# Gathers of two edge attentions released chunk by chunk, norm stages ordered by tile, a placing step with two digits

## The chip, the cores and the metric

The kernel runs on one core of one Trainium2 chip. The metric is the device time of one execution in microseconds (us); less is better. The engines are named as in the profile: PE (TensorE, with PEld for its weight loads), DVE (VectorE), ACT (ScalarE), POOL (GpSimd) and SP (the queue that issues most DMAs). A suffix q (SPq, POOLq) means an instruction of the engine's queue that occupies no data path.

## The reference

A graph of 3125 nodes with 256 features each; the edges are 25000 random pairs in both directions and one loop per node, 53125 in all, sorted by target. Four layers, each as `x = layernorm(x + f(x))`:

```python
# layer 0: attention, 8 heads; scores from text embeddings, values from x
scores = sum(Q[col] * (K[row] + rel)) / sqrt(32);  attn = softmax over the edges of each target
out = segment_sum(attn * V[row]) @ Wo.T + bo
# layer 1: attention, 4 heads; score = leaky(alpha_src[src] + alpha_dst[dst])
h = segment_sum(softmax(score) * val[src])
# layer 2: 5 GIN layers  (segment_sum(relu(h[src])), two products, two batch norms each)
# layer 3: 3 SAGE layers (mean over neighbours, two products)
```

All inputs and the output are float32.

## The kernel before

The program is a row of phases. Each is closed by a barrier of all engines (class Phase), and within one each engine runs its own list of instructions in order, with waits on semaphores written by hand. The order is: prepare, find_windows, attend_edges and merge_parts for layer 0, residual_norm (norm 0), tables_layer1, attend_edges for layer 1, merge_parts, residual_norm (norm 1), GIN, norm 2, SAGE, norm 3.

**attend_edges** (from L554; once per attention). The edges are cut into 416 chunks of 128, and 8 chunks make one of 52 groups. A buffer `from_src` holds the gathered rows of RING = 4 groups. For each chunk POOL issues one indirect DMA (L682) that brings the 128 source rows from HBM: 2 KB a row in layer 0 (values and keys), 1056 B in layer 1 (values and alphas). SP loads a window of 128 target rows for each chunk (L663). A function `tick` on each engine handles one group g, and the steps of neighbouring groups are interleaved:

- PE sums the eight chunks of group g - 1 (`sum_parts`, L854 and L856: values and weights times a one-hot matrix) into two PSUM buffers that alternate by chunk. ACT copies each sum out (L945, L947), and PE may start chunk j only when ACT has copied chunk j - 2. The last matmul of a chunk increments `chunk_summed[b]`, b being the buffer of the group.
- PE turns the scores of group g (L835), DVE runs two scans for the largest score of each target (L734, L737), PE turns the result back (L841), DVE subtracts (L746, L749), ACT takes the exponent (L929, L930), and DVE weights the gathered values (L753).
- DVE makes the one-hot matrices of group g + 2 (L695, L696), PE turns them (L805), ACT copies them (L922).
- PE spreads the target rows of group g + 1 to its edges (L827). In layer 0 DVE multiplies them by the gathered keys (`match`, L707) and reduces to scores (L719); in layer 1 it adds the alphas (L725, L728).
- In layer 1 DVE, PE and ACT count the edges into an adjacency matrix beside it (L769, L771, L869, L960).

POOL has only the gathers there. For group g it waits once, for the eighth chunk of group g - 4, whose buffer it reuses, and then issues eight gathers in one block:

```python
for g in range(NG):
    b = g % RING
    pool.wait_ge(chunk_summed[b], G * (g // RING) + 1)
    for j in range(G):
        nc.gpsimd.indirect_dma_start(...).then_inc(src_in[b], 16)
```

The waits for the first four groups are met at the start. A gathered group is first read two ticks after the tick in which its gathers are released.

**prepare** (from L84). A loop over 25 node tiles makes the tables of layer 0 on PE (L369). In the same loop each edge chunk's target number is placed into a table of parts: DVE makes one-hots of the tile (`is_tile`, L297) and of the row (`is_row`, L301) for 16 chunks, POOL multiplies the first by the digits of the target number (`tile_digits`, L211), and PE multiplies the two (L358). The number is carried as three float16 digits: number / 64, number mod 64, and a flag for a part that spans chunks.

**residual_norm** (from L1310; four times). 25 tiles of 128 nodes in five slabs of five tiles. For a slab, x is summed with what is added (norm 0: the attention's result turned and multiplied by Wo, L1527, L1468, L1535; norms 2 and 3: the turned h_t, turned back by PE, L1497), DVE takes the statistics (L1418, L1421, L1423), ACT the square root (L1449), DVE the shift (L1429, L1431), ACT normalises (L1454), and PE and ACT turn the result (L1506, L1460). In norm 0 PE also makes the alphas (L1513). Each engine handles one step for a whole slab before the next step: PE, for example, projects the tiles of slab s + 2, then turns out slab s, then makes the alphas of slab s - 1. The order on ACT is root(s + 1), copy_more(s + 2), normalise(s), copy_turned(s).

## Time and profile before

| | |
|---|---|
| time, median of 3 runs (lowest to highest) | 4185.14 us (4184.43 to 4191.37) |
| the profiled execution's own time | 4209.37 us |
| its span, first to last instruction | 4207.7 us, 54657 instructions |
| PE busy | 3086.4 us (73%) |
| DVE, ACT, POOL busy | 1658.5, 1079.9, 1138.7 us |
| phases: prepare, find_windows | 0 to 188, to 272 |
| attention 0, merge, norm 0, tables of layer 1 | to 1270, 1326, 1431, 1490 |
| attention 1, merge, norm 1 | to 2482, 2553, 2593 |
| GIN, norm 2, degrees, SAGE, norm 3 | to 3548, 3596, 3603, 4172, 4207 |

Times in the profile are us from the first instruction unless marked ns. A row in order of time has the start, the duration, the engine, the line, the operation, output <- inputs and how many were merged (xN), and in brackets the idle time of the engine before it and what ended it. What ended a wait is inferred from the semaphores, and where a number of a semaphore is used again in another phase the name can be that of an old transfer. A row of busy time has the stretch and its length, then the busy us (and instructions) of PE, PEld, DVE, ACT and POOL, then the clock that PE was granted as a share of 2.4 GHz, the mean busy share of the core's 16 DMA engines, and GB/s moved. The end of a matmul in the profile is modelled from its size; it is not the time at which other engines see its result. The page also lists, by line, the time spent busy, the mean of one instruction, and the idle time before it.

### The profile page before, as it was taken

Reading aid. Unit: us, or ns where it says so; the run is one execution under the profiler, and the core shown is the slowest. Engines: PE = TensorE matmul, PEld = TensorE weight load, DVE = VectorE, ACT = ScalarE, POOL = GpSimd, SP = SyncE. Lnnn points to the kernel's source line nnn. Section 1 sums busy time; section 2 is a strip of 40 time slices with the busy share of each in tenths; the row PEclk is TensorE's granted clock in tenths of the full one; section 3 lists DMA queues with packets and bytes.
Section 4 is the critical chain, followed back from the end, with each engine's and each line's share of the span. In section 5 each row is a group of like instructions: output and inputs, shape, how many; then the busy total and the mean of one; then the engine's idle time right before and its main releaser. Section 6 shows DMA issues by size and latency. Waiting matters only on the chain. (4 is left out here: it accounts for less than half of the span.)

```text
span 4207.7 us, 54657 instructions
## 1 busy us (share of the span) xinstructions
PE 3086.4 (73%) x17789; PEld 2267.0 (54%) x17789; DVE 1658.5 (39%) x2726; ACT 1079.9 (26%) x2952; POOL 1138.7 (27%) x1072
## 2 busy tenths in 40 slices
PE   5306666666675646666666675999999997799997
PEld 4305565565563536655565663555555564455554
DVE  8725455455554134444444444141323324302112
ACT  0002233233331224443443433030322313201001
POOL 6563443434433243434434321000000000101010
PEclk8758888888886667777877776999999998899998
DMA  5255555555543134444544334424233240433331
GB/s 205 63 168 155 175 172 160 176 160 175 173 128 101 47 77 83 77 78 88 84 83 79 78 56 143 153 91 134 92 105 113 89 144 0 146 114 101 102 131 42
DMA packets 330861, 477.67 MB, mean 114 GB/s; under 512 B 148534, under 2 KB 241414, under 8 KB 329940
## 3 DMA queue, kind: packets, MB, share of 16 engines
q1 hardware_dynamic: 271492, 297.49, 25.4%
q0 software_dynamic: 59088, 176.67, 14.7%
q8 instruction: 148, 2.42, 0.2%
q14 instruction: 133, 1.09, 0.1%
HBM read 417.29 MB, written 58.52 MB: 113 GB/s over the span
## 5 line engine op out<-in xcount | busy, mean ns | idle before, releaser
L854 PE MATMUL e_part_ps<-e_onehot,e_from_src 128*128 128x129 f32 x3328 | 674.5, 335 | 601.3 <-ACT ends L947 349.0
L854 PEld LDWEIGHTS e_part_ps<-e_onehot,e_from_src 128*128 128x128 f32 x3328 | 560.5, 235 | 678.3 <-ACT ends L947 391.6
L945 ACT ACTIVATE sums<-e_part_ps 128x384 f32 x832 | 410.3, 493 | 1115.9 <-PE e_part_ps L856 356.8
L682 POOL DMA_INDIRECT e_from_src<-vk,src x416 | 394.3, 948 | 583.4 <-PE e_part_ps L856 454.1
L682 POOL DMA_INDIRECT e_from_src<-val,src x416 | 394.4, 948 | 578.9 <-PE e_part_ps L856 444.5
L2060 PE MATMUL gin_sum_ps<-slab,high 128*128 128x391 f16 x2000 | 497.7, 330 | 2.5 <-DMA slab<-adj 1.8
L2060 PE MATMUL gin_sum_ps<-slab,low 128*128 128x391 f16 x2000 | 497.4, 330 | 0.0
L827 PE MATMUL e_spread_ps<-e_window,e_onehot_t 128*128 128x256 f32 (+1 forms) x1664 | 346.8, 346 | 63.8 <-DMA e_window<-q_part 28.7
L856 PE MATMUL e_part_ps<-e_onehot,e_small 128*65 128x129 f32 x1664 | 382.3, 318 | 0.0
L827 PEld LDWEIGHTS e_spread_ps<-e_window,e_onehot_t 128*128 128x128 f32 x1664 | 269.2, 208 | 85.2 <-issue 41.6
L1754 PE MATMUL sage_sum_ps<-slab,high 128*128 128x391 f16 x1200 | 301.1, 333 | 11.7 <-DVE z_t L1877 6.4
L1754 PE MATMUL sage_sum_ps<-slab,low 128*128 128x391 f16 x1200 | 301.3, 333 | 0.0
L2060 PEld LDWEIGHTS gin_sum_ps<-slab,low 128*128 128x128 f16 x2000 | 195.0, 97 | 139.4 <-issue 1.8
L734 DVE TENSOR_TENSOR_SCAN e_fixed<-link,e_turn_ps 64x128 f32<-64x128 bf16 x104 | 43.8, 421 | 568.2 <-DMA out<-pr_zero 492.5
L2060 PEld LDWEIGHTS gin_sum_ps<-slab,high 128*128 128x128 f16 x2000 | 194.9, 98 | 131.2 <-DVE low L2229 4.6
L856 PEld LDWEIGHTS e_part_ps<-e_onehot,e_small 128*65 128x65 f32 x1664 | 257.3, 167 | 0.0
L753 DVE TENSOR_TENSOR e_from_src<-e_from_src,e_fixed 128x2048 f32<-128x2048 f32 x104 | 237.9, 2288 | 43.2 <-ACT e_fixed L929 41.6
L2122 POOL TENSOR_SCALAR h_t<-h_t 128x391 f32<-128x391 f32 x32 | 39.7, 1251 | 780.3 <-DVE h_t L2267 780.3
L2237 DVE SCALAR_TENSOR_TENSOR z_t<-h_t,gin_own,gin_sum_ps 128x391 f32<-128x391 f32 x80 | 44.8, 617 | 490.1 <-PE gin_sum_ps L2060 490.1
L2131 ACT ACTIVATE gin_y_t<-gin_proj_ps,gin_columns 128x391 f32<-128x391 f32 x80 | 46.8, 585 | 572.6 <-PE gin_proj_ps L2073 572.6
L707 DVE TENSOR_TENSOR e_from_src<-e_from_src,e_spread_ps 128x512 f32<-128x512 f32 x208 | 140.5, 675 | 121.4 <-PE e_spread_ps L827 105.0
L1877 DVE TENSOR_TENSOR z_t<-sage_sum_ps,inv_degree_all 128x391 f32<-128x391 f32 x48 | 23.8, 558 | 364.3 <-PE sage_sum_ps L1754 364.3
(282 smaller groups left out, 4255.4 us busy)
## 6 DMA issues: line engine op xcount, KB each, us to landing
slab<-adj SPq DMA_DIRECT2D x160, 977.5 KB, 4.8
e_window<-q_part SPq DMA_DIRECT2D x416, 128.0 KB
adj<-e_counts SPq DMA_DIRECT2D x8, 1250.0 KB
adj<-e_counts SPq DMA_DIRECT2D x8, 1193.8 KB
e_from_src<-vk,src POOLq DMA_INDIRECT x416
e_from_src<-val,src POOLq DMA_INDIRECT x416
e_window<-alpha_part SPq DMA_DIRECT2D x416, 4.0 KB
vk<-pr_out SPq DMA_DIRECT2D x25, 256.0 KB, 2.0
```

What stands on the lines that cost most here:

```text
L682: nc.gpsimd.indirect_dma_start(from_src[:, b, j, :], None, by_src, bass.IndirectOffsetOnAxis(ap=keep["src"][:, g * G + j:g * G + j + 1], a ...
L707: nc.vector.tensor_tensor(k_rows, k_rows, spread_ps[pair % 2][:, :].rearrange("p (j d) -> p j d", j=2), ALU.mult).then_inc(used[pair % 2], 1)
L734: nc.vector.tensor_tensor_scan(running, keep["link"][:, g, 0:P], turned, -FAR, ALU.add, ALU.max).then_inc(fwd, 1)
L753: nc.vector.tensor_tensor(from_src[:, b, :, 0:D].rearrange("p j (h d) -> p j h d", h=H), from_src[:, b, :, 0:D].rearrange("p j (h d) -> p ...
L827: mm = nc.tensor.matmul(to, onehot_t[:, r, j, :], window[:, r, j, :], start=True, stop=True)
L854: nc.tensor.matmul(part_ps[s][:, k * ENDS:(k + 1) * ENDS], from_src[:, b, j, k * P:(k + 1) * P], onehot[:, b, j, :], start=True, stop=True)
L856: nc.tensor.matmul(part_ps[s][0:SMALL, KH * ENDS:(KH + 1) * ENDS], small[:, r, j, :], onehot[:, b, j, :], start=True, stop=True).then_inc( ...
L945: nc.scalar.activation(keep["sums"][:, :, bass.ds(starts[j], P)], of[:, :, 0:P], ACT.Copy).then_inc(whole_copied, 1)
L1754: mm = nc.tensor.matmul(sum_ps[KH * n + m][:, 0:AN], part[:, t, m * P:(m + 1) * P], slab[:, s, n, k * AN:(k + 1) * AN], start=(t == 0 and ...
L2060: mm = nc.tensor.matmul(sum_ps[KH * n + m][:, 0:AN], part[:, t, m * P:(m + 1) * P], slab[:, s, n, k * AN:(k + 1) * AN], start=(t == 0 and ...
L2131: nc.scalar.activation((z_t if p else y_t)[:, m, cols(b)], proj_ps[v % (2 * KH)][:, 0:AN], ACT.Identity, bias=columns[:, 3 * p, m:m + 1], ...
L2237: nc.vector.scalar_tensor_tensor(out=z_t[:, m, cols(b)], in0=h_t[:, m, cols(b)], scalar=own[:, l:l + 1], in1=sum_ps[KH * n + m][:, 0:AN], ...
```

## The change

In `attend_edges`, each gather waits for the sum of its own chunk in the group four back, not once for the last of the eight. In `prepare`, the flag is added to the second digit as 64, two digits are multiplied and placed, and the flag is taken out again afterwards by one comparison and one subtraction. In `residual_norm`, PE, ACT and DVE go tile by tile: PE and ACT bring in tile t + 7 (SLAB + AHEAD) between the steps of tile t, the copy of a turned tile follows the normalising of the next, the alphas follow by tile, and DVE takes the statistics of a tile right after its sum, the bias being added to the slab ahead of it; the shift of slab s - 1 is made after the second tile of slab s. In norm 1, where nothing is turned in, the sum stays by slab and the shift of slab s - 1 comes before it.

```diff
-            pool.wait_ge(half_sem, 5)
+            pool.wait_ge(half_sem, 4)
             for u in range(STEPS):
                 cols = slice(u * STEP, (u + 1) * STEP)
                 if u >= 2:
                     pool.wait_ge(placed, u - 1)
                 pool.wait_ge(tiles_spotted, u + 1)
                 nc.gpsimd.tensor_tensor(tile_digits[:, u % 2, :, :, :],
-                                        is_tile[:, u % 2, :, :].unsqueeze(2).to_broadcast([P, STEP, 3, TW]),
-                                        digits[:, cols, :].unsqueeze(3).to_broadcast([P, STEP, 3, TW]), ALU.mult).then_inc(digits_spotted, 1)
+                                        is_tile[:, u % 2, :, :].unsqueeze(2).to_broadcast([P, STEP, 2, TW]),
+                                        digits[:, cols, :].unsqueeze(3).to_broadcast([P, STEP, 2, TW]), ALU.mult).then_inc(digits_spotted, 1)
...
-            nc.vector.tensor_copy(digits[:, :, 1], ints[:, 5, :]).then_inc(half_sem, 1)
...
-            nc.vector.tensor_tensor(spans[:, 0, :], spans[:, 0, :], spans[:, 1, :], ALU.add).then_inc(spanned, 1)
+            nc.vector.tensor_tensor(spans[:, 0, :], spans[:, 0, :], spans[:, 1, :], ALU.max).then_inc(spanned, 1)
             v.wait_ge(spanned, 5)
-            nc.vector.tensor_tensor(digits[:, :, 2], spans[:, 0, :], keep["first"][:, :], ALU.mult).then_inc(half_sem, 1)
+            nc.vector.scalar_tensor_tensor(out=spans[:, 0, :], in0=spans[:, 0, :], scalar=64.0, in1=keep["first"][:, :],
+                                           op0=ALU.mult, op1=ALU.mult).then_inc(spanned, 1)
+            v.wait_ge(spanned, 6)
+            nc.vector.tensor_tensor(digits[:, :, 1], spans[:, 0, :], ints[:, 5, :], ALU.add).then_inc(half_sem, 1)
...
+            nc.vector.tensor_scalar(part_number[:, 2, :], part_number[:, 1, :], 63.5, None, ALU.is_gt).then_inc(node_sem, 1)
+            v.wait_ge(node_sem, 3)
+
+            nc.vector.scalar_tensor_tensor(out=part_number[:, 0, :], in0=part_number[:, 2, :], scalar=-64.0,
+                                           in1=part_number[:, 0, :], op0=ALU.mult, op1=ALU.add).then_inc(node_sem, 1)
+            v.wait_ge(node_sem, 4)
...
-                    mm = nc.tensor.matmul(node_ps[:, 0:3 * TW], is_row[:, u % 2, j, :],
+                    mm = nc.tensor.matmul(node_ps[:, 0:2 * TW], is_row[:, u % 2, j, :],
...
             for g in range(NG):
-                b = g % RING
-
-                pool.wait_ge(chunk_summed[b], G * (g // RING) + 1)
+                b, it = g % RING, g // RING
                 for j in range(G):
+
+                    if it:
+                        pool.wait_ge(chunk_summed[b], G * (it - 1) + j + 2)
                     nc.gpsimd.indirect_dma_start(
                         from_src[:, b, j, :], None, by_src,
                         bass.IndirectOffsetOnAxis(ap=keep["src"][:, g * G + j:g * G + j + 1], axis=0)).then_inc(src_in[b], 16)
...
+            def add_tile(t):
+
+                if by_tile:
+                    v.wait_ge(in_turned, t + 1)
+                    nc.vector.tensor_tensor(x[:, t, :], x[:, t, :], in_ps[t % IN][:, 0:D], ALU.add).then_inc(summed, 1)
+                v.wait_ge(summed, t + 1 if by_tile else t // SLAB + 1)
+                nc.vector.bn_stats(stats[:, t, :], x[:, t, :]).then_inc(stat, 1)
...
-            take_stats(0)
-            for s in range(1, NSLAB):
-                take_stats(s)
-                make_shift(s - 1)
+            for s in range(NSLAB):
+                if s and not by_tile:
+                    make_shift(s - 1)
+                add_slab(s)
+                for t in tiles(s):
+                    add_tile(t)
+                    if s and by_tile and t % SLAB == AHEAD - 1:
+                        make_shift(s - 1)
+                close_slab(s)
...
+            if weight is not None:
+                for t in range(SLAB + AHEAD):
+                    copy_more(t)
+            for s in range(NSLAB):
+                root(s)
                 for t in tiles(s):
-                    nc.scalar.activation(x[:, t, :], x[:, t, :], ACT.Identity, bias=shift[:, t:t + 1],
-                                         scale=std[:, t:t + 1]).then_inc(normed, 1)
-
-            def copy_turned(s):
-                for t in tiles(s):
-                    act.wait_ge(out_turned, t + 1)
-                    nc.scalar.activation(turned_to[:, :, t * P:(t + 1) * P], out_ps[t % OUT][:, 0:D].rearrange("p (k n) -> p k n", k=KH),
-                                         ACT.Copy).then_inc(out_copied, 1)
-
-            def copy_more(s):
-                for t in tiles(s):
-                    act.wait_ge(more_turned, t + 1)
-                    if t >= 2:
-                        act.wait_ge(in_turned, t - 1)
-                    nc.scalar.activation(more_t[:, t % 2, :, :], turn_ps[t % 2][:, 0:D].rearrange("p (k n) -> p k n", k=KH),
-                                         ACT.Copy).then_inc(more_copied, 1)
-
-            if weight is not None:
-                copy_more(0)
-                copy_more(1)
-            root(0)
-            for s in range(NSLAB):
-                if s + 1 < NSLAB:
-                    root(s + 1)
+                    normalise(t)
+                    if turned_to is not None and t % SLAB:
+                        copy_turned(t - 1)
+                    if weight is not None and t + SLAB + AHEAD < NT and t % SLAB < SLAB - AHEAD:
+                        copy_more(t + SLAB + AHEAD)
+                if turned_to is not None:
+                    copy_turned(t)
                 if weight is not None and s + 2 < NSLAB:
-                    copy_more(s + 2)
-                normalise(s)
-                if turned_to is not None:
-                    copy_turned(s)
+                    for u in range(AHEAD):
+                        copy_more((s + 2) * SLAB + u)
...
+            def bring_in(t):
+
+                if t >= NT:
+                    return
+                if added_t is not None:
+                    turn_in(t)
+                elif weight is not None:
+                    if t + 1 < NT:
+                        turn_more(t + 1)
+                    project_in(t)
...
-            if added_t is not None:
-                turn_in(0)
             if weight is not None:
                 pe.wait_ge(w_in, 16)
-                project_in(0)
-                project_in(1)
+                turn_more(0)
+            for t in range(SLAB + AHEAD):
+                bring_in(t)
             for s in range(NSLAB):
-                if added_t is not None and s + 1 < NSLAB:
-                    turn_in(s + 1)
-                if weight is not None and s + 2 < NSLAB:
-                    project_in(s + 2)
-                if turned_to is not None:
-                    turn_out(s)
-                if alpha_to is not None and s > 0:
-                    make_alpha(s - 1)
+                for t in tiles(s):
+                    if turned_to is not None:
+                        turn_out(t)
+                    if t % SLAB < SLAB - AHEAD:
+                        bring_in(t + SLAB + AHEAD)
+                    if alpha_to is not None and t:
+                        make_alpha(t - 1)
+                for u in range(AHEAD):
+                    bring_in((s + 2) * SLAB + u)
             if alpha_to is not None:
-                make_alpha(NSLAB - 1)
+                make_alpha(NT - 1)
```

## Rows read from the trace of the kernel before

**Rows 1.** Busy time by stage (us; instructions in brackets), TensorE's clock, DMA share, GB/s:

```profile
0.00:188.00 188.00, 97.57 (x728) 78.15 (x728) 159.41 (x153) 0.00 (x0) 118.91 (x40) 0.86 0.42 144
...
1326.00:1431.00 105.00, 69.58 (x300) 56.86 (x300) 30.91 (x95) 32.30 (x82) 0.00 (x0) 0.68 0.31 99
...
3548.00:3596.00 48.00, 24.62 (x100) 17.34 (x100) 23.18 (x90) 21.62 (x55) 0.00 (x0) 0.57 0.00 0
...
4172.00:4207.00 35.00, 11.35 (x50) 8.30 (x50) 22.18 (x90) 13.76 (x30) 0.00 (x0) 0.53 0.27 92
...
400.00:1230.00 830.00, 563.70 (x3287) 490.22 (x3284) 417.33 (x530) 254.30 (x842) 338.06 (x357) 0.84 0.55 170
...
1600.00:2430.00 830.00, 543.65 (x3851) 499.04 (x3852) 381.79 (x492) 341.33 (x989) 335.19 (x354) 0.76 0.48 83
```

**Rows 2.** Costliest groups: busy, mean ns | idle before them, and its releasers:

```profile
L682 POOL DMA_INDIRECT e_from_src<-vk,src x416 | 394.3, 948 | 583.4 <-PE e_part_ps L856 454.1
...
L734 DVE TENSOR_TENSOR_SCAN e_fixed<-link,e_turn_ps 64x128 f32<-64x128 bf16 x104 | 43.8, 421 | 568.2 <-DMA out<-pr_zero 492.5
```

**Rows 3.** Order of time, one group of the second attention (start, us, engine, line):

```profile
1912.63 0.94 POOL L682 DMA_INDIRECT e_from_src<-val,src  x1 [8.39 <-PE e_part_ps L856]
...
1914.35 0.66 PE L854 MATMUL e_part_ps<-e_onehot,e_from_src 128*128 128x129 f32 x4
...
1914.79 0.22 DVE L725 TENSOR_TENSOR e_raw_score<-e_from_src,e_spread_ps 128x64 f32<-128x64 f32 x1 [1.66 <-PE e_spread_ps L827]
...
1915.07 0.61 PE L854 MATMUL e_part_ps<-e_onehot,e_from_src 128*128 128x129 f32 x4
...
1915.74 0.27 PE L835 MATMUL e_turn_ps<-ident,e_score 128*64 128x128 f32 x1
...
1921.41 0.95 POOL L682 DMA_INDIRECT e_from_src<-val,src  x1 [0.30 <-issue]
...
1924.22 0.49 ACT L945 ACTIVATE sums<-e_part_ps 128x384 f32 x1 [3.75 <-remote]
...
1924.25 0.42 DVE L734 TENSOR_TENSOR_SCAN e_fixed<-link,e_turn_ps 64x128 f32<-64x128 bf16 x1 [8.98 <-DMA out<-pr_zero]
```

**Rows 4.** Busy time around those gathers, and in a group without gathers:

```profile
1912.60:1913.90 1.30, 1.30 (x14) 1.30 (x15) 0.53 (x1) 0.72 (x4) 0.97 (x2) 1.00 0.03 1
...
1913.90:1924.00 10.10, 2.11 (x23) 1.84 (x22) 0.45 (x2) 1.35 (x2) 6.62 (x7) 0.86 0.43 109
...
1924.00:1932.60 8.60, 7.62 (x58) 7.13 (x58) 5.88 (x8) 5.54 (x17) 0.00 (x0) 0.77 0.03 2
...
334.00:343.40 9.40, 9.40 (x72) 8.43 (x71) 9.15 (x13) 4.67 (x15) 0.00 (x0) 1.00 0.37 114
```

**Rows 5.** Order of time, the next group's first two sums copied by ACT:

```profile
1936.96 0.49 ACT L945 ACTIVATE sums<-e_part_ps 128x384 f32 x1 [1.96 <-PE e_part_ps L856]
...
1941.27 0.49 ACT L945 ACTIVATE sums<-e_part_ps 128x384 f32 x1 [3.75 <-DMA x<-x]
```

**Rows 6.** Order of time, DVE and POOL in the first stage's loop:

```profile
30.71 0.64 DVE L297 TENSOR_TENSOR pr_is_tile<-pr_iota,pr_tile_of 128x464 f16<-128x464 f16 x1
...
46.76 4.45 POOL L211 TENSOR_TENSOR pr_tile_digits<-pr_is_tile,pr_digits 128x1392 f16<-128x1392 f16 x1 [0.64 <-DVE pr_is_tile L297]
...
49.67 2.03 DVE L297 TENSOR_TENSOR pr_is_tile<-pr_iota,pr_tile_of 128x464 f16<-128x464 f16 x1
...
51.85 4.45 POOL L211 TENSOR_TENSOR pr_tile_digits<-pr_is_tile,pr_digits 128x1392 f16<-128x1392 f16 x1 [0.64 <-DVE pr_is_tile L297]
```

**Rows 7.** Order of time, norm 0, the first projection of two slabs:

```profile
1356.44 2.07 PE L1535 MATMUL n_in_ps<-n_w_out,n_more_t 128*128 128x256 f32 x4 [4.78 <-ACT n_more_t L1468]
...
1373.09 2.08 PE L1535 MATMUL n_in_ps<-n_w_out,n_more_t 128*128 128x256 f32 x4 [4.78 <-ACT n_more_t L1468]
```

**Rows 8.** Order of time, norm 2, DVE's first sums of two slabs:

```profile
3562.72 2.13 DVE L1409 TENSOR_TENSOR x<-x,n_in_ps 128x256 f32<-128x256 f32 x5 [4.57 <-PE n_in_ps L1497]
...
3572.15 2.13 DVE L1409 TENSOR_TENSOR x<-x,n_in_ps 128x256 f32<-128x256 f32 x5 [4.57 <-PE n_in_ps L1497]
```

More of the change, by code:

```diff
@@ L1352, in residual_norm @@
         loads = (add is not None) + (x_from is not None)
+        by_tile = added_t is not None or weight is not None
+        AHEAD = 2
         block = ctx.enter_context(nc.Block(f"norm{layer}"))
@@ L1416, in take_stats, with close_slab @@
                     v.wait_ge(biased, s + 1)
-                for t in tiles(s):
-                    nc.vector.bn_stats(stats[:, t, :], x[:, t, :]).then_inc(stat, 1)
+                if not by_tile:
+                    nc.vector.tensor_tensor(x[:, slab, :], x[:, slab, :], more[:, slab, 0:D], ALU.add).then_inc(summed, 1)
+            def close_slab(s):
+                slab = slice(s * SLAB, (s + 1) * SLAB)
                 v.wait_ge(stat, SLAB * (s + 1))
@@ L1539, in _, with turn_in, turn_more @@
-            if added_t is not None:
-                turn_in(0)
+            def turn_in(t):
+                if t >= IN:
+                    pe.wait_ge(summed, t - IN + 1)
+                for k in range(KH):
+                    mm = nc.tensor.transpose(in_ps[t % IN][:, k * P:(k + 1) * P], added_t[:, k, t * P:(t + 1) * P], keep["ident"][:, :])
+                mm.then_inc(in_turned, 1)
+            def turn_more(t):
+                if t % SLAB == 0:
+                    pe.wait_ge(loaded[t // SLAB], 16 * loads)
+                if t >= 2:
+                    pe.wait_ge(more_copied, t - 1)
+                for k in range(KH):
+                    mm = nc.tensor.transpose(turn_ps[t % 2][:, k * P:(k + 1) * P], more[:, t, k * P:(k + 1) * P], keep["ident"][:, :])
+                mm.then_inc(more_turned, 1)
```

103 lines of the change are left out of this document (43 added, 60 removed).

## The prediction, made before the result was known

> **What bounds the kernel now.** First the busy time by stage [rows 1]. The two attentions take 998 and 992 us of the 4207.7 us span, and in them no engine is near full: in 830 us of the first PE is busy 563.7, DVE 417.3, ACT 254.3, POOL 338.1. In that window POOL issues 357 gathers, 44.6 groups of eight: one group per 18.6 us; in 830 us of the second, 354 gathers: one per 18.8 us. Next the costliest groups of instructions [rows 2]: in the first attention alone POOL waits 454.1 us for PE's chunk sums, so PE holds the gathers back, and DVE is idle 568.2 us before its first scan, 492.5 of it put down to a releaser that cannot be the right one (a store of zeros done long before). So I went to the order of time in one group [rows 3]. The gathers start at 1912.63. PE sums a chunk from 1914.35 and the next from 1915.07, 0.7 us a chunk, and turns the scores at 1915.74 for 0.27 us. DVE needs only that, but its scan starts at 1924.25, 8.2 us later; ACT, which should copy the first sum out at about 1915.3, starts at 1924.22. Both start 1.9 us after the last gather instruction has ended (1921.41 + 0.95). The busy times of the same stretches [rows 4] say what lasts until then: for 1.3 us after the first gather's start the DMA share is 0.03, then for 10.1 us it is 0.43 and PE is busy 2.1 us, DVE 0.45, ACT 1.35; then the share is 0.03 again and in 8.6 us PE does 7.6. So while the data of gathers arrives, PE's finished results are hardly seen by DVE, ACT and POOL. A few slip through: in the next group ACT copies the first sum at 1936.96, in the midst of the gathers, and the second only at 1941.27 [rows 5]. A group without gathers takes 9.4 us, and PE is busy in all of it at the full clock of 2.4 GHz [rows 4]. So a group of today is 9.4 us of work and then about 10 us of gathers, nearly one after the other: 9.4 + 10.1 = 19.5 against 18.7 measured.
>
> The Trainium skill, page "SBUF — State Buffer", section "Who interferes with whom", says that DMA never contends with a compute engine. By that rule the wait has another cause and it does not matter when a gather is in flight. The rows disagree in time at least: PE's results come out when the traffic ends. I weigh the rule as the first rival below.
>
> **The change, part by part.**
>
> *Gathers one chunk at a time (both attentions).* The same 416 gathers each, none added; a gather now waits for the sum of its own chunk four groups back, not for the eighth. The first four groups need no wait, as before, and the last three have no gathers behind them, so 48 periods per attention change, 96 in all. POOL gains seven waits a group; it queues nothing else there, and no consumer is near: the gathered group is used two groups later. So an earlier gather is worth nothing by itself. What changes is that eight gathers in one block become several short ones between the sums. Take each block with its sums as a round. PE's results are seen up to about 2 us after a gather's start (1.3 us until traffic, and DVE's L725 started 2.2 us after it [rows 3]); after the last gather of the block they are all seen. One gather's data takes (1924.0 - 1913.9) / 8 = 1.26 us, and its tail ends 2.8 us after its start (1.9 + 0.95). Let two sums be seen at time 0. Gathers start at 0 and 1.25. ACT copies the first sum out (0.49 + 0.17), PE needs 0.7 for the next, so a third sum is done at about 1.4: seen, and a third gather joins. The fourth, after ACT's second copy, is done at about 2.0 to 2.2: even chance. The fifth is not seen before the block ends at 2.5 + 2.8 = 5.3 (with the fourth inside: 6.6). A round of three sums in 5.3 us is 14.1 us for eight, of two in 4.05 us (third missed) 16.2, of four in 6.6 us 13.2. To that come the results that are not sums: turned scores, turned peaks, spread windows, turned one-hots; each that falls into a block is late by what is left of it, at most about 3 us now instead of 8.2, but DVE's 9.4 us of work in a group (417.3 / 44.6 [rows 1]) must fit around them. Also PE falls to 1.2 GHz now and then (clock 0.84 and 0.76 of full [rows 1]), which stretches 9.4 us of work. I add 1 to 2 us to the 14.1 and take 15.7 us. Gain: 18.7 - 15.7 = 3.0 us x 96 = 288 us. The ends: PE's own work, 9.4 us a group, would give 9.3 x 96 = 893 us; eight blocks of one, none beside any work, would cost 9.4 + 8 x 1.5 = 21.4 us (a single gather's stall taken as its tail less the free head, 2.8 - 1.3), 2.7 x 96 = 259 us more than now. I stay near the middle, since the row of the first 2 us and the rows of the rest of the block are from the same kernel and only their order is new.
>
> *Two digits in place of three (prepare).* The loop turns once in 5.09 us (POOL L211 at 46.76 and 51.85 [rows 6]), 25 times. DVE's is_tile takes 0.64 us before POOL runs at all and 2.03 beside it, ending at 51.70, 0.5 us after POOL's 46.76 + 4.45 = 51.21: it waits for POOL's multiply, and POOL's next waits for it: 4.45 + 0.64 = 5.09. With 928 in place of 1392 elements I take POOL at two thirds, 2.97 us, so 3.61 us a turn; DVE's own work is 5.09 - 2.03 + 0.64 = 3.70, and that binds next. PE has 97.6 us in the whole stage [rows 1], 3.9 a turn at most. I take 3.85: gain 1.24 x 25 = 31 us. Ends: 36 (3.64), and 15 if POOL has a fixed part. The two added small DVE operations ahead of the loop lie beside DVE's wait for inputs; the two behind it cost 0.4 us.
>
> The Trainium skill, same page, section "SBUF: two separate sides", calls the port pair that DVE and GpSimd share an exclusive lock held for the whole instruction. The 0.5 us between POOL's end and is_tile's end agree with it; by a split of bandwidth instead, the loop would still be bound by POOL and the sum the same.
>
> *Norm 0 by tile.* A slab of five tiles takes 16.65 us (PE L1535 at 1356.44 and 1373.09 [rows 7]), and in each PE waits 4.78 us for ACT, which stands in its queue at the square root that DVE makes ready; DVE then waits for PE's last tile behind five turns. The same instructions are now interleaved by tile, seven tiles ahead. PE has 69.6 us in the 105, at a clock of 0.68. I take PE's wait away in four slabs (19 us) and at the end, where turns and alphas follow the last five tiles, two tiles of PE's work (69.6 / 25 = 2.8 us each): 25 us. Ends: 36 (PE never idle) and 5.
>
> *Norm 2* takes 9.43 us a slab [rows 8], with DVE idle 4.57 of it behind normalise, turn, copy, turn in. DVE's own 4.9 us and about 1 us for the waits on its own results by tile give 6.7: gain 2.7 x 4 = 11 us (3 to 16). *Norm 3* has no turning back; DVE has 22.2 of 35 us; 3 us (0 to 6). *Norm 1* moves only the order of ACT and PE, and what it waits for is its loads: nothing, 3 us either way.
>
> **Sum.** 288 + 31 + 25 + 11 + 3 = 358 us off the profiled execution's 4209.4 us, 3851 us. That execution is 24.2 us (0.58%) above the median 4185.1, so by the same factor: 3830 us.
>
> **Rivals.**
> *A: order does nothing in the attentions.* What is late is late because eight gathers have to pass in a period, whenever they do; the period stays 18.7. For it: the work and the traffic add up today to nearly the period, and the page's rule above. Against it: idle engines beside short blocks have what to do, and today's block is idle because it is long. Time: (4209.4 - 70) x 0.994 = 4115 us.
> *B: the overlap is nearly full.* Results come through between short blocks, as one did at 1936.96; the period goes to 11 to 14 us, where DVE's 9.4 and PE's 9.4 us bind. At 12.8: 5.9 x 96 = 566, time 3550 us.
> *C: slower.* Each gather, released by its own sum, makes its own stall, just as the results that the next sum needs are due: the place is ACT's copy between a sum and the sum two further on. Eight stalls with nothing beside them give 21.4 us: 4209 - 70 + 259 = 4398, by the same factor 4373 us. It decides from a period of 18.7 + 70 / 96 = 19.4 us on. For it: traffic would then cover nearly all of the period, where today 8.6 us are quiet, and PE may lose its clock in many short idle times (at 1.2 GHz its 9.4 us are 18.8). Against it: PE and ACT can always go one pair of sums further while one gather lands, and the other stages give 70 us in any case.
>
> **How the numbers follow.** Forecast (period 14.2 to 17.3, 3690 to 3985 us) 0.50; A and between (17.3 to 19.4) 0.21; B 0.18; C 0.09; within 0.2% of before 0.02. A measurement of this kernel tells about 0.2% from no change. The range 3610 to 4130 us takes in all of A and the upper part of B (a period from 13.4 us on), and leaves out C. Faster 0.89, same 0.02, slower 0.09.
>
> **What would show it.** Right: gathers start at uneven distances, two to four together; the scan L734's idle time falls from 5.5 us each (568.2 us over 104 [rows 2]) to under 3; the period of L682 by eights is near 15.7; DMA share in the attentions rises by a fifth with the same bytes; L211 near 3 us and its distance 3.85; norm 0 near 80 us. Wrong: if the stalls are not tied to traffic, ACT and DVE would again start together once a group; and if PE's clock in the attentions falls below 0.7, C is the case.

## The result: 3600 us, a gain 1.6 times the forecast, the excess all in the attentions

The changed kernel takes 3600.32 us (median of 4 runs, 3586.49 to 3608.12) against 4185.03 us: a ratio of 0.8596, interval 0.8568 to 0.8624. The forecast was 3830 us, the range 3610 to 4130. Its profiled execution took 3598.55 us, with a span of 3596.8 us. From barrier to barrier in the two profiles:

| stage | before, us | after, us | gain | forecast |
|---|---|---|---|---|
| prepare | 187.9 | 171.8 | 16.1 | 31 |
| attention 0 | 997.4 | 703.6 | 293.8 | 144 |
| attention 1 | 992.3 | 731.8 | 260.5 | 144 |
| norm 0 | 105.4 | 76.0 | 29.4 | 25 |
| norm 1 | 39.2 | 40.8 | -1.6 | 0 |
| norm 2 | 47.8 | 39.7 | 8.1 | 11 |
| norm 3 | 35.4 | 34.9 | 0.5 | 3 |
| the rest | 1801.8 | 1797.8 | 4.0 | 0 |

Busy time by stage in the profile after (stretch, its length, busy us of PE, PEld, DVE, ACT, POOL, TensorE's clock, DMA share, GB/s); it answers [rows 1]:

```profile
0.00:172.00 172.00, 90.69 (x728) 71.84 (x728) 138.64 (x155) 0.00 (x0) 98.40 (x40) 0.86 0.47 158
1016.00:1092.00 76.00, 52.75 (x300) 45.58 (x300) 32.63 (x95) 32.23 (x82) 0.00 (x0) 0.81 0.44 137
400.00:900.00 500.00, 422.56 (x2923) 359.44 (x2922) 367.04 (x471) 228.80 (x750) 298.55 (x316) 1.00 0.81 250
1200.00:1800.00 600.00, 488.06 (x3901) 446.83 (x3901) 384.58 (x495) 340.92 (x994) 338.22 (x359) 0.89 0.66 112
```

In the first attention 316 gathers fall into 500 us: 12.66 us for eight, where it was 18.6. PE is busy 0.85 of the time instead of 0.68, and its granted clock went from 0.84 to 1.00; in the second attention from 0.76 to 0.89. The DMA share of the first attention went from 0.55 to 0.81, a rise by a half with the same bytes where a fifth was forecast, as the period fell by more than was forecast. The costliest groups after; they answer [rows 2]:

```profile
L690 POOL DMA_INDIRECT e_from_src<-vk,src x416 | 393.1, 945 | 290.7 <-PE e_part_ps L864 184.3 <-issue 86.1 <-POOLq L74 16.9
...
L690 POOL DMA_INDIRECT e_from_src<-val,src x416 | 393.0, 945 | 318.5 <-PE e_part_ps L864 219.6 <-issue 75.7 <-POOLq L74 20.5
...
L742 DVE TENSOR_TENSOR_SCAN e_fixed<-link,e_turn_ps 64x128 f32<-64x128 bf16 x104 | 43.8, 421 | 131.0 <-PE e_turn_ps L843 76.7 <-issue 37.7 <-DMA out<-pr_zero 16.6
```

The scan's idle time is 1.3 us each instead of 5.5. The order of time in one group of the first attention after (start, us, engine, line) shows how; it answers [rows 3, 5]:

```profile
685.86 0.95 POOL L690 DMA_INDIRECT e_from_src<-vk,src  x1 [1.47 <-PE e_part_ps L864]
...
686.09 0.27 PE L843 MATMUL e_turn_ps<-ident,e_score 128*64 128x128 f32 x1
...
686.40 0.42 DVE L742 TENSOR_TENSOR_SCAN e_fixed<-link,e_turn_ps 64x128 f32<-64x128 bf16 x1 [0.83 <-issue]
...
687.11 0.95 POOL L690 DMA_INDIRECT e_from_src<-vk,src  x1 [0.30 <-issue]
...
687.60 0.38 PE L864 MATMUL e_part_ps<-e_onehot,e_small 128*65 128x129 f32 x2
...
688.36 0.95 POOL L690 DMA_INDIRECT e_from_src<-vk,src  x1 [0.30 <-issue]
...
690.18 0.49 ACT L953 ACTIVATE sums<-e_part_ps 128x384 f32 x1 [2.25 <-PE e_part_ps L864]
...
690.33 0.95 POOL L690 DMA_INDIRECT e_from_src<-vk,src  x1 [1.02 <-PE e_part_ps L864]
...
691.58 0.95 POOL L690 DMA_INDIRECT e_from_src<-vk,src  x1 [0.30 <-issue]
...
692.84 0.95 POOL L690 DMA_INDIRECT e_from_src<-vk,src  x1 [0.30 <-issue]
...
695.01 0.94 POOL L690 DMA_INDIRECT e_from_src<-vk,src  x1 [1.23 <-PE e_part_ps L864]
```

The scores turned at 686.09 are scanned at 686.40: at once. The sum that PE ended at 687.98 (687.60 + 0.38) is copied at 690.18, 2.2 us late. So the hold (PE has finished a result, and the other engines see it late) is still there, but a block has two or three gathers (685.86, 687.11, 688.36; then 690.33, 691.58, 692.84). POOL goes on 1.97 and 2.17 us after the last start of a block, 0.7 and 0.9 us more than the 1.25 us inside a block.

In prepare, norm 0 and norm 2 the periods are read in the same way; they answer [rows 6, 7, 8]:

```profile
40.95 3.65 POOL L211 TENSOR_TENSOR pr_tile_digits<-pr_is_tile,pr_digits 128x928 f16<-128x928 f16 x1 [0.64 <-DVE pr_is_tile L299]
...
45.25 3.66 POOL L211 TENSOR_TENSOR pr_tile_digits<-pr_is_tile,pr_digits 128x928 f16<-128x928 f16 x1 [0.65 <-DVE pr_is_tile L299]
...
1036.97 0.60 ACT L1473 ACTIVATE x<-x,n_shift,n_std 128x256 f32<-128x256 f32 x1 [2.87 <-DVE n_shift L1445]
...
1049.26 0.60 ACT L1473 ACTIVATE x<-x,n_shift,n_std 128x256 f32<-128x256 f32 x1 [2.95 <-DVE n_shift L1445]
...
2957.36 0.42 DVE L1412 TENSOR_TENSOR x<-x,n_in_ps 128x256 f32<-128x256 f32 x1 [1.84 <-PE n_in_ps L1518]
...
2964.33 0.42 DVE L1412 TENSOR_TENSOR x<-x,n_in_ps 128x256 f32<-128x256 f32 x1 [1.84 <-PE n_in_ps L1518]
```

### The profile page after: what moved, and what is told of

It is laid out like the page before. It is cut to its first block and busy times, and to the rows that moved or that the text cites. A ratio compares the mean times of both kernels' runs of the same rounds, so it can differ in the third digit from the quotient of the medians.

```text
span 3596.8 us, 54659 instructions
## 1 busy us (share of the span) xinstructions
PE 2896.4 (81%) x17789; PEld 2083.4 (58%) x17789; DVE 1637.8 (46%) x2728; ACT 1081.6 (30%) x2952; POOL 1115.2 (31%) x1072
## 5 line engine op out<-in xcount | busy, mean ns | idle before, releaser
L862 PE MATMUL e_part_ps<-e_onehot,e_from_src 128*128 128x129 f32 x3328 | 588.4, 302 | 177.0 <-issue 95.4
L862 PEld LDWEIGHTS e_part_ps<-e_onehot,e_from_src 128*128 128x128 f32 x3328 | 473.4, 202 | 252.3 <-issue 136.8
L835 PE MATMUL e_spread_ps<-e_window,e_onehot_t 128*128 128x256 f32 (+1 forms) x1664 | 325.9, 330 | 101.8 <-DMA e_window<-q_part 39.0
L864 PE MATMUL e_part_ps<-e_onehot,e_small 128*65 128x129 f32 x1664 | 337.3, 286 | 0.0
L835 PEld LDWEIGHTS e_spread_ps<-e_window,e_onehot_t 128*128 128x128 f32 x1664 | 258.2, 203 | 129.7 <-issue 76.3
L761 DVE TENSOR_TENSOR e_from_src<-e_from_src,e_fixed 128x2048 f32<-128x2048 f32 x104 | 237.6, 2284 | 18.5 <-issue 12.4
L864 PEld LDWEIGHTS e_part_ps<-e_onehot,e_small 128*65 128x65 f32 x1664 | 222.2, 147 | 0.0
L1783 PEld LDWEIGHTS sage_sum_ps<-slab,high 128*128 128x128 f16 x1200 | 117.1, 98 | 89.8 <-issue 13.8
```

Of the source, the lines that this page charges most:

```text
L761: nc.vector.tensor_tensor(from_src[:, b, :, 0:D].rearrange("p j (h d) -> p j h d", h=H), from_src[:, b, :, 0:D].rearrange("p j (h d) -> p ...
L835: mm = nc.tensor.matmul(to, onehot_t[:, r, j, :], window[:, r, j, :], start=True, stop=True)
L862: nc.tensor.matmul(part_ps[s][:, k * ENDS:(k + 1) * ENDS], from_src[:, b, j, k * P:(k + 1) * P], onehot[:, b, j, :], start=True, stop=True)
L864: nc.tensor.matmul(part_ps[s][0:SMALL, KH * ENDS:(KH + 1) * ENDS], small[:, r, j, :], onehot[:, b, j, :], start=True, stop=True).then_inc( ...
L1783: mm = nc.tensor.matmul(sum_ps[KH * n + m][:, 0:AN], part[:, t, m * P:(m + 1) * P], slab[:, s, n, k * AN:(k + 1) * AN], start=(t == 0 and ...
```

## The experiments

The runs fell on four chips, and that matters: on chips 7, 8 and 4 the kernel before takes 4183 to 4216 us, as on the chip of the first profiles, and on chip 11 3382 us. One number is used throughout, the lateness: how long after the modelled end of the last matmul of a chunk's sum its semaphore is incremented, in the first attention (third quartile over the 416 sums; where records of increments are missing, the next one is taken). In the kernel before it is 2.9 us, after the change 1.4 us. The median in the kernel before is 0.01 us, since more than half of the sums are seen at once. The number shows that there is a hold; it is not a price, since a sum made earlier also waits longer. "Period" is the distance of gathers by eights.

| run | chip | us | kernel before there | ratio, interval | period 0, 1 | lateness, us |
|---|---|---|---|---|---|---|
| e1_release_only | 11 | 3360.1 | 3381.7 | 0.9943, 0.9926 to 0.9961 | 10.1, 10.7 | 0.01 |
| e2_rest_only | 11 | 3326.6 | 3381.7 | 0.9844, 0.9828 to 0.9861 | 10.6, 10.8 | 0.01 |
| e3_pairs | 11 | 3317.0 | 3381.7 | 0.9807, 0.9785 to 0.983 | 10.1, 10.7 | 0.01 |
| e4_fours | 11 | 3319.1 | 3381.7 | 0.9813, 0.979 to 0.9836 | 10.2, 10.9 | 0.01 |
| e8_changed_again | 7 | 3605.5 | 4182.7 | 0.8618, 0.8601 to 0.8635 | 12.7, 13.4 | 1.4 |
| e9_release_only | 7 | 3650.7 | 4187.6 | 0.8723, 0.8681 to 0.8766 | 12.6, 13.2 | 1.6 |
| e18_rest_only | 4 | 4166.7 | 4215.9 | 0.9881, 0.9859 to 0.9902 | 18.6, 18.6 | 2.9 |
| e5_pauses | 7 | 3609.9 | 4182.7 | 0.863, 0.8607 to 0.8654 | 13.2, 13.5 | 1.3 |
| e10_pairs | 7 | 3628.3 | 4187.6 | 0.8662, 0.864 to 0.8685 | 12.7, 13.8 | 1.7 |
| e11_fours | 7 | 3714.6 | 4187.6 | 0.887, 0.8831 to 0.8908 | 13.8, 14.4 | 0.9 |
| e12_short_pauses | 7 | 3631.7 | 4187.6 | 0.8657, 0.8624 to 0.8689 | 13.3, 13.8 | 1.6 |
| e6_thin | 7 | 4127.7 | 4182.7 | 0.9868, 0.9841 to 0.9895 | 18.5, 18.3 | 2.1 |
| e14_half_rows | 8 | 4165.4 | 4189.7 | 0.994, 0.9921 to 0.996 | 18.6, 18.6 | 2.8 |
| e15_direct | 8 | 3701.8 | 4189.7 | 0.8834, 0.8816 to 0.8852 | none | 0.01 |
| e7_none | 7 | 3356.3 | 4182.7 | 0.8024, 0.8002 to 0.8046 | none | 0.01 |
| e13_third_buffer | 8 | 3604.3 | 4189.7 | 0.8604, 0.8578 to 0.8629 | 12.5, 13.5 | 2.4 |
| e16_two_pauses | 4 | 3719.7 | 4215.9 | 0.8829, 0.881 to 0.8847 | 15.0, 13.9 | 2.2 |
| e17_two_pauses_third | 4 | 3653.0 | 4215.9 | 0.8653, 0.8625 to 0.8682 | 13.5, 14.1 | 1.5 |

**The parts alone, and other block sizes.** In the kernel before, the wait of each gather alone (e1, e9); in the changed kernel, the wait of the block alone (e2, e18), or a wait for each two or four chunks (e3, e10 and e4, e11). The edit of the pairs:

```diff
+                    if it and j % 2 == 0:
+                        pool.wait_ge(chunk_summed[b], G * (it - 1) + j + 3)
```

> The kernel before with the chunk-by-chunk release alone. In the profiles the two attentions went from 997 and 992 us to 704 and 732 us, 554 us together, while the stages around them gave 57 us. Theory P (pauses): PE's results reach the other engines in the pauses between short blocks of gathers, and the release alone makes these; so the attentions are as in the changed kernel, within 10 us each, and the time is 4185 - 554 = 3631 us, 3610 to 3650. Rival Q: a part of the 554 us comes from what the other parts of the change leave behind (PE's clock, granted 0.82 and 0.76 before and 0.96 and 0.87 after); then the time is over 3700 us.

> The changed kernel with the gathers released in blocks of eight again: prepare and the norms are as changed. Theory P: the attentions are as in the kernel before, 990 to 1000 us each, and the 57 us of the other stages remain: 4185 - 57 = 4128 us, 4118 to 4138. Rival Q: the attentions too are shorter than before, by 50 us or more together, and the time is under 4080 us.

> The changed kernel with a release for each two chunks (after the sum of the second). Theory P: the blocks hold two or four gathers; a block of two makes a round of 1.25 + 2.2 = 3.5 us (14.0 us for eight), a block of four one of 3.75 + 2.2 = 6.0 us (12.0 us); a period of 12.5 to 14.0 us against 12.6 and 13.3 in the changed kernel, a time of 3600 to 3700 us. Rival R (what pays is that a gather follows its own sum at once): each doubling of the block costs about a third of the way back to 18.6 us, so 14.6 us and 3790 us or more.

> The changed kernel with a release for each four chunks. Theory P: two blocks of four in a group; what PE may sum ahead of ACT's copies is two chunks, so after each block about two more sums must be made before the next one: 3.75 + 2.2 + 1.4 = 7.3 us, 14.7 us a period (14 to 16), attentions of about 800 us, a time of 3750 us (3690 to 3870). Rival S (what is held back is in proportion to the gathers in flight, however they are cut): what separates the changed kernel from the one before is not the number of pauses, and fours stay close to eights: over 17 us, over 3980 us.

All four missed, since chip 11 has no hold. Busy time and order of time of e2_rest_only there, blocks of eight:

```profile
300.00:800.00 500.00, 493.70 (x3496) 426.78 (x3495) 432.92 (x565) 268.17 (x898) 358.37 (x379) 1.00 0.92 298
```

```profile
703.51 0.95 POOL L689 DMA_INDIRECT e_from_src<-vk,src  x1 [0.30 <-issue]
...
704.04 0.38 PE L863 MATMUL e_part_ps<-e_onehot,e_small 128*65 128x129 f32 x2
...
704.54 0.49 ACT L952 ACTIVATE sums<-e_part_ps 128x384 f32 x1 [1.67 <-PE e_part_ps L863]
...
704.76 0.94 POOL L689 DMA_INDIRECT e_from_src<-vk,src  x1 [0.30 <-issue]
```

The sum that ended at 704.42 is copied at 704.54, in the midst of eight gathers; 379 gathers take 500 us, 10.6 us for eight, and PE is busy 0.99 of it. There the release moves the kernel by 0.6% (e1), the other parts by 1.6% (e2). The changed kernel was then run again, unedited:

> The changed kernel once more. The four runs so far ran on another chip than the two profiles: there the kernel before takes 3382 us, its attentions 561 and 592 us, and no result of PE is held back. Theory H (the hold belongs to the chip, and the change's gain in the attentions exists only where the hold does): where the kernel before takes about 3382 us, the changed one takes 3310 to 3330 us, a ratio of 0.980 to 0.985; where it takes about 4185 us, 3590 to 3610, 0.860. Rival T (the first profiles were of some passing condition, not of a chip): a ratio between these, or 4185 us on the chip of the first four runs.

(The 561 us there is the first attention of e1; with blocks of eight it is 578.) On chip 7 the ratio is 0.862, as at first. Theory H stands as far as it was tried; the changed kernel itself was not run on chip 11. The same edits on chips with the hold:

> The kernel before with the chunk-by-chunk release alone, wanted on a chip with the hold (kernel before near 4185 us). Theory P: the attentions take 704 and 736 us as in the changed kernel, so 4185 - 550 = 3635 us (3620 to 3660). Rival Q (the other parts help the attentions): over 3700 us. On a chip without the hold: 3360 us, as measured there.

> The changed kernel with the gathers released in blocks of eight, wanted on a chip with the hold (kernel before near 4185 us), where only variants of it have run so far. Prepare and the norms alone: attentions 990 to 1000 us each, 4185 - 57 = 4128 us, 4118 to 4138. Rival Q (these parts change the attentions too): under 4080 us.

Attentions of 702 and 729 us with the release alone (3650.7 us, as P said), 997 and 995 us without it (e18). So the whole gain of the attentions is the release's: 4187.6 - 3650.7 = 537 us; the other parts gave 49 us on chip 4. The time of e18, 4166.7, lies above the 4138 of the expectation, because the kernel before took 4215.9 us on that chip, 31 us more than on the first; the attentions are as expected.

> The changed kernel with a release for each two chunks, wanted on a chip with the hold. There, blocks of eight with three pauses of 1.0 us had a period of 13.2 us in which POOL never waited. Theory P: blocks of two and four, 12.3 to 13.5 us a group, 3590 to 3680 us. Rival R (the own sum): 14.6 us and 3790 us or more. On a chip without the hold: 3317 us, as measured there.

> The changed kernel with a release for each four chunks, wanted on a chip with the hold. Theory P: two blocks of four; after each, two more sums have to be made before the next one: 3.75 + 2.2 + 1.4 = 7.3 us, 14.7 us a group (14 to 16), 3800 us (3730 to 3930). Rival S (held time in proportion to the gathers, however they are cut): over 17 us, over 4000 us. On a chip without the hold: 3319 us, as measured there.

Pairs came as P said in time (3628) and in the first attention; the second has 13.8 us, 0.3 above P's range. Fours were better than P (3715 against 3730 to 3930): all 96 blocks of each attention are of four, but in the first attention only one of the two pauses of a group is long, 3.9 us from start to start in the median, and the other 2.4 us. S is out.

**Pauses without the release.** The edit is that of e5. Groups of eight, released at the eighth sum as before, but POOL fills a small buffer of its own three times (e5) or twice (e12) after the second, fourth and sixth gather, or three times after the third and sixth (e16), the last also with a third PSUM buffer for the sums of layer 0 (e17):

```diff
+                    if j % 2 == 1 and j < G - 1:
+                        for _ in range(3):
+                            nc.gpsimd.memset(idle[:, 0:256], 0.0).then_inc(idled, 1)
+                            n_idle += 1
+                            pool.wait_ge(idled, n_idle)
```

> The changed kernel with blocks of eight, and POOL idling about 1.1 us (three small fills of a buffer of its own) after the second, fourth and sixth gather. Theory P: on a chip with the hold PE's results come through in these pauses, so that the period falls from 18.6 to 15 to 17 us although POOL does 3.3 us more in each group: 3780 to 3980 us against 4128 for blocks of eight. Rival R (it is the release after the own sum that pays): the period grows to 21.9 us, 4440 us. On a chip without the hold both say POOL's 10.0 us and 3.3 us more, 13.3 us a group: 3326 + 96 x 3.0 = 3610 us.

> The changed kernel with blocks of eight and POOL idling 0.7 us (two small fills) after the second, fourth and sixth gather, where three fills gave a pause of 1.03 us, a period of 13.2 us and 3610 us. Theory P1 (POOL's own time binds, a pause of 0.7 us lets enough through): 10.0 + 3 x 0.7 = 12.1 us, 3610 - 96 x 1.0 = 3515 us. Theory P2 (results get through only behind a gap of about 1 us): the short pauses are lost, 19 to 21 us a group, over 4100 us. Between them (some pauses fail): 13 to 16 us. On a chip without the hold 12.1 us and 3520 us by all.

POOL in e5, first attention:

```profile
503.17 0.95 POOL L692 DMA_INDIRECT e_from_src<-vk,src  x1 [0.27 <-POOL e_idle L697]
504.43 0.95 POOL L692 DMA_INDIRECT e_from_src<-vk,src  x1 [0.30 <-issue]
505.37 1.06 POOL L697 MEMSET e_idle<- 128x256 f32 x3
506.70 0.95 POOL L692 DMA_INDIRECT e_from_src<-vk,src  x1 [0.27 <-POOL e_idle L697]
507.96 0.95 POOL L692 DMA_INDIRECT e_from_src<-vk,src  x1 [0.30 <-issue]
509.21 0.95 POOL L692 DMA_INDIRECT e_from_src<-vk,src  x1 [0.30 <-issue]
```

This is the run that decides. POOL does 3.1 us more in each group, and the kernel is 573 us faster than the one before, as fast as the changed one; between two groups (507.96 to 509.21) POOL does not wait, as at 45 of the 48 group ends of the first attention and 36 of the second, so the eighth sum is done in time although no gather was released early. R is out. P predicted 3780 to 3980 and forecast too little, like the prediction itself. Pauses of 0.66 us more than the 1.26 us (e12) lose a part: in the first attention POOL waits again before half of the groups (24 of 48), 3.9 us from start to start on the mean, and the period is 13.3, not 12.1 (P1) and not 19 (P2).

> The changed kernel with blocks of eight and POOL idling 1.03 us (three fills) after the third and the sixth gather: two pauses in place of three. Wanted on a chip with the hold. With three pauses POOL never waited in the first attention (13.2 us = 8 x 1.25 + 3 x 1.03 + 0.1) and the time was 3610 us. Theory P1 (two pauses are still enough to get all results out): 12.1 us a group, 3610 - 80 = 3530 us, a version better than the changed kernel. Rival F (each pause lets about two sums through, so two pauses and the end are too few): POOL waits before each group again, 13.5 to 16 us, 3640 to 3880 us. On a chip without the hold 12.1 us, 3520 us.

> The same with three PSUM buffers for the chunk sums of layer 0. Theory P1: POOL is the bound in both, so within 10 us of the run with two pauses. Rival F: with blocks of three and three buffers three sums go through each pause in layer 0, its attention falls to 12.1 us a group (about 670 us) while layer 1 stays: 40 to 90 us under the run with two pauses.

> The changed kernel with three PSUM buffers in place of two for the chunk sums of layer 0 (layer 1 has no room), so that PE may sum three chunks ahead of ACT's copies. Wanted on a chip with the hold. Theory P (a pause ends when the sum that POOL waits for has been made and seen, and PE is stopped in a block by its two buffers): PE has three sums ready at a pause, blocks of three to four, the first attention's period falls from 12.66 to 11.5 to 12.2 us, 25 to 55 us in all, so 3550 to 3580 us. Rival B (the blocks are ended by other waits, and two buffers were not what stopped PE): within 8 us of 3603 us. On a chip without the hold POOL's 10.0 us bind: 3310 to 3330 us by both.

Two pauses are too few (F): in layer 0 POOL waits before half of the groups (24 of 48), 7.1 us from start to start on the mean, and the period is 15.0 us. With the third buffer it falls to 13.5 us, the attention from 800 to 728 us and the time by 67 us, as F said (40 to 90); F's 12.1 us and 670 us were not reached, and layer 1, where nothing was changed, went from 13.9 to 14.1 us. So in layer 0 what one pause lets through is limited in part by the two sums that PE may have ready. Where the release times the pauses itself (e13) a third buffer gave 10 us in that attention and nothing in the time: there three pauses come of themselves, and B holds. None of these beat the changed kernel.

**What in a gather holds PE's results.** Edits of the kernel with blocks of eight, from the fifth group on: rows cut to an eighth (e6), half the rows (e14), direct loads by SP of as many rows of the same length, but adjacent ones (e15), nothing (e7). All four leave the values of real sources out.

```diff
-                        from_src[:, b, j, :], None, by_src,
+                        from_src[:, b, j, 0:wide], None, table,        # e6: wide = ws // 8
...
+                    sp.dma_start(from_src[:, b, j, :], by_src[at:at + P, :]).then_inc(direct_in[b], 16)   # e15
```

> The changed kernel with blocks of eight, where from the fifth group on a gather brings only the first eighth of each row (256 and 132 bytes in place of 2048 and 1056), as many rows as before; the values used are old ones. Theory N (what holds PE's results back goes with the number of rows or with POOL's issuing, not with bytes; the two layers have the same period, 18.6 us, with rows of 2048 and 1056 bytes): on a chip with the hold the period stays 18 to 19 us, 4100 to 4150 us. Rival D (it is the data's own traffic): the period falls to 10.6 to 13 us, 3350 to 3600 us. On a chip without the hold POOL's 10.0 us bind: 3300 to 3330 us by both.

> The changed kernel with blocks of eight, where from the fifth group on each gather brings 64 rows in place of 128, of full length; the values used for the rest are old ones. Wanted on a chip with the hold (an eighth of the bytes at 128 rows changed nothing there: 4128 us). Theory N1 (the hold goes with the number of rows in flight): half the rows leave the queue idle for half of each gather's 1.25 us, results get through, a period of 10.6 to 14 us, 3370 to 3700 us. Rival N2 (it goes with POOL's issuing, whatever it issues): 18 to 19 us, 4100 to 4150 us. On a chip without the hold 3300 to 3330 us by both.

Busy time of e6, e14 and e18 in the first attention, in this order:

```profile
400.00:1200.00 800.00, 542.75 (x3176) 473.51 (x3175) 403.45 (x517) 247.39 (x814) 323.55 (x343) 0.84 0.27 71
```

```profile
400.00:1200.00 800.00, 548.95 (x3169) 476.06 (x3167) 402.40 (x513) 246.26 (x809) 309.45 (x344) 0.81 0.42 114
```

```profile
400.00:1200.00 800.00, 546.53 (x3176) 475.31 (x3174) 403.31 (x513) 246.21 (x811) 324.07 (x342) 0.83 0.55 169
```

The DMA share falls from 0.55 to 0.27 and 0.42, and the work of PE, DVE and ACT in 800 us is the same within 2%. The instruction also takes as long for 64 rows as for 128 (0.90 against 0.95 us). So N and N2: neither bytes nor rows count. What is left is POOL's issuing of the gather, which takes as long in all three. With half the rows ACT sees the next sum 2.95 us after the last start, as before the change (2.8 us in [rows 3]):

```profile
505.91 0.90 POOL L690 DMA_INDIRECT e_from_src<-vk,src  x1 [0.30 <-issue]
...
508.86 0.49 ACT L953 ACTIVATE sums<-e_part_ps 128x384 f32 x1 [5.12 <-DMA fw_a_cols<-in_L_gnn_a]
```

> The changed kernel where from the fifth group on SP loads 128 rows that lie together (direct DMAs, eight in a block after the eighth sum of the group four back, same bytes and rows of the same length) in place of POOL's gathers; the values are of other rows. Wanted on a chip with the hold. Theory K (the hold belongs to POOL's software queue): no result is held back, attentions near the 585 and 602 us without gathers, at most 700 us if SP's own issuing binds, 3360 to 3570 us. Rival D2 (any traffic of that many rows into the same buffer holds PE's results back): 16 us a group and more, over 3900 us.

```profile
648.54 3.65 SPq L680 DMA_DIRECT2D e_from_src<-vk  x8
...
650.93 0.38 PE L873 MATMUL e_part_ps<-e_onehot,e_small 128*65 128x129 f32 x2
...
651.43 0.49 ACT L962 ACTIVATE sums<-e_part_ps 128x384 f32 x1 [1.81 <-PE e_part_ps L873]
```

The same bytes arrive (228 GB/s in the first attention), and a sum ended at 651.31 is copied at 651.43. K's mechanism holds as far as this goes, no result is late; its number does not: 3702 against 3360 to 3570. SP loads the windows behind the rows now, and in 600 us PE waits 120 us for a window (the attentions take 748 and 782 us). D2 said over 3900. Two things changed at once here, the issuer (SP for POOL) and the rows (adjacent for scattered); no run issued direct loads from POOL, so which of the two ends the hold was not separated.

> The changed kernel without the gathers of all groups but the first four; the later groups use old rows. What is left is the work of the other engines, which is the same on every chip: 9.4 to 10.1 us a group, attentions of 490 to 530 us, 3326 - 1170 + 1020 = 3176 us, 3130 to 3230. Theory H: the same on a chip with the hold and on one without. Rival W (PE, DVE or ACT themselves are slower on a chip with the hold): over 3300 us there.

```profile
400.00:800.00 400.00, 399.79 (x2912) 356.48 (x2911) 363.41 (x473) 223.03 (x746) 0.00 (x0) 1.00 0.36 106
```

Without gathers PE is busy all the time at 2.4 GHz, 10.1 us a group, and the attentions take 585 and 602 us; with gathers on chip 11 they take 578 and 593. So the engines are as fast there within 1.5% and W is out, though the time (3356) lies over its bound: the 9.4 to 10.1 us a group of the expectation left out the first and last groups and layer 1's counting. What the hold and POOL's gathers still cost the changed kernel is 704 - 585 and 732 - 602, 249 us in all.

## Why the forecast was wrong

*What bounds the kernel:* right. Eight gathers in a block, with PE's results out only behind it; e5, e9 and e15 show it three ways. The words "while the data of gathers arrives" were not: e6 and e14 change the data, and the hold stays. The work was put too low as well: 9.4 us a group came from a window of 9.4 us, and without gathers a group takes 10.1 us (e7).

*The mechanism of the gain:* right. Blocks of two and three were forecast; of the 140 blocks of the first attention 46 have two gathers and 80 have three.

*The step that failed* is the price of a round, "2.5 + 2.8 = 5.3" us for three sums, and the 1 to 2 us added to it. The 2.8 us from the last start of a block to the moment at which its results are seen came from one block of eight [rows 3] and was used for blocks of two and three. It is not a constant. The semaphore records of the first attention give, from the start of a block's last gather to the next increment by PE (median): 1.6 us after blocks of two (45), 1.8 after three (80), 1.9 after four (10) and 2.1 after five (2) in the kernel after, 1.9 after four in e11 and 2.7 after eight in the kernel before. So each gather more in a block made the tail some 0.2 us longer. POOL went on 2.1 us after the last start in the median (690.33 - 688.36 and 695.01 - 692.84 are two of them). That alone makes 2.5 + 2.1 = 4.6 us for three, 12.3 us for eight, where 14.1 stood; 12.6 was measured. The rest is the addition: results other than sums were to be late by what is left of a block, and PE's clock was to stretch the work. The scan is preceded by 1.3 us of idle time, beside PE's other work, and the granted clock was 1.00 in the first attention and 0.89 in the second. So 15.7 became 12.6 and 13.3 us: (18.6 - 12.6) x 48 + (18.6 - 13.3) x 48 = 542 us instead of 288. The trace of before held a hint: in [rows 5] one result came out in mid-block, and the prediction left it to rival B.

*Rivals.* B was the case (11 to 14 us), with a chance of 0.18; its price at 12.8 us, 3550 us, was 50 us too low. A is refuted: it is the order that counts (e5, e9). The Trainium skill's rule beside it, "SBUF — State Buffer", section "Who interferes with whom", says that DMA never contends with a compute engine. e15 agrees for direct DMAs (0.01 us at the third quartile); for POOL's gathers the kernel before on a chip with the hold does not: PE computes on until its buffers are full, but the other engines see its results 2.9 us later. The page also says that a DMA that seems stalled by a DVE instruction is one whose descriptors GpSimd writes, and that issuing it from the hardware queue ends that. No run here shows that case, where the DMA is the one that waits; here PE's results wait, and in e15, with SP issuing, they did not. C is refuted by the result itself and by e9.

*Prepare:* direction right, size not. POOL's multiply went from 4.45 to 3.65 us for two thirds of the elements, not to 2.97: (4.45 - 3.65) / 464 = 1.7 ns an element and 2.05 us that do not shrink. The turn is 3.65 + 0.65 = 4.30 us, 0.79 less, times 25 = 20 us; the barrier came 16 earlier. The lower end, 15, was this case.

*The shared port:* is_tile ends 0.5 us after POOL again in each turn, and nothing here tells a lock from a split.

*Norms:* norm 0 has 12.29 us a slab instead of 16.65 and gave 29 of 25. Norm 2 has 6.97 us a slab (6.7 forecast) and gave 8 of 11; the terms that the prediction names for it, 4.9 and about 1 us, add up to 5.9 and not to 6.7, so the near hit is partly luck. Norm 3 gave 0.5 of 3. Norm 1 lost 1.6 us, within the 3 us allowed.

*Sum without the attentions:* forecast 70 us, measured 56.5 in the profiles and 49 on chip 4.

## What to carry to other kernels

If all engines but one resume together just after POOL's last gather, look at when results are seen, not at the sizes of transfers, and cut the block: two or three gathers, then a gap of 2 us from start to start. What a gap lets through is at most what PE has ready, so look at its output buffers (a third one gave 67 us in e17 and nothing in e13). And time a kernel on several chips before pricing such a stall: the change is worth 14% where the hold is, and its main part 0.6% where it is not.

## What was not expected of the hardware

- Chips differ: one kernel takes 3382 us on one and 4183 to 4216 us on three. What was seen to differ in the profiles is the lateness of PE's results while POOL issues gathers (0.01 against 2.9 us at the third quartile in blocks of eight). The stage tables_layer1, with 29 gathers, differs too: 44 us against 57. GIN, which has no gathers, takes 957 to 961 us on both kinds. What in the chips makes this was not found.
- The hold has one direction. In the kernel before PE turns a group's scores 0.9 to 1.1 us (median) after DVE has ended them, in the midst of POOL's block, but DVE's scan starts 2.9 us (first attention) and 7.5 us (second) after that turn; in e2, without the hold, 0.6 and 0.04 us.
- Inside a block of eight results come through one by one: from 2 us after its first start to the end of its last gather mostly one to three increments by PE in the first attention of the kernel before, and mostly 11 or 12 in e2. PE also makes fewer there, since it is stopped.
- The lateness went with POOL's gather instructions: it stayed with an eighth of the bytes and with half the rows, was gone with as many adjacent rows loaded by SP, and POOL's fills do not cause it (e5).
- An indirect DMA cost POOL 0.90 us for 64 rows and 0.94 to 0.95 for 128, with rows of 132 to 2048 bytes, and the next one started 0.30 us later.
